# Moving a product with C from GpSimd to VectorE in a 16-layer Mamba kernel, with the five engines' lists reordered

## The reference, cut to what matters

```python
H, I, N, R, K, NL = 192, 384, 16, 48, 4, 16      # width, channels, states, dt rank, conv taps, layers
def selective_scan(u, dt, A, Bm, Cm, Dp):
    def step(h, inp):
        u_t, dt_t, B_t, C_t = inp
        dA = jnp.exp(dt_t[:, :, None] * A)
        h = dA * h + (dt_t * u_t)[:, :, None] * B_t[:, None, :]
        y = jnp.einsum('bin,bn->bi', h, C_t)
        return (h, y)
    ...
    return jnp.moveaxis(ys, 0, 1) + u * Dp
def mamba_layer(x, p):
    h = rmsnorm(x, nw)
    u, z = jnp.split(jnp.einsum('blh,ch->blc', h, in_w), 2, axis=-1)
    u = jax.nn.silu(causal_conv(u, cw, cb))
    proj = jnp.einsum('bli,ci->blc', u, xp_w)
    dt_r, Bm, Cm = (proj[..., :R], proj[..., R:R + N], proj[..., R + N:])
    dt = jax.nn.softplus(jnp.einsum('blr,ir->bli', dt_r, dtw) + dtb)
    y = selective_scan(u, dt, -jnp.exp(a_log), Bm, Cm, dp) * jax.nn.silu(z)
    return x + jnp.einsum('bli,hi->blh', y, ow)
```

## Time and profile before

| what | value |
|---|---|
| time, median of 3 runs | 14570.39 us (14560.91 to 14575.47) |
| the profiled execution's own time | 14539.11 us |
| its span | 14537.1 us |
| mean granted TensorE clock | 0.929 of full |
| stage of the layers | about 200 us to 13412 us of the span |
| VectorE, GpSimd, TensorE, ScalarE busy | 89%, 87%, 87%, 78% of the span |

### The profile page before, as it was taken

How to read it: one execution, slowest core, us unless ns; L and a number is a source line. 1 busy time by engine, 2 the same in 40 slices (tenths; PEclk the granted TensorE clock), 3 DMA queues, 4 the chain that set the end, 5 groups by cost and what they waited for, 6 DMA issues and landing times. The chain is left out here.

```text
span 14537.1 us, 203073 instructions
## 1 busy us (share of the span) xinstructions
PE 12640.6 (87%) x51466; PEld 6492.0 (45%) x51466; DVE 12997.2 (89%) x8757; ACT 11405.9 (78%) x21744; POOL 12668.3 (87%) x6352
## 2 busy tenths in 40 slices
PE   7888888888888888888888888888888888888989
PEld 4444444444444444444444444444444444444767
DVE  3999999999999999999999999999999999998633
ACT  4888888888888888888888888888888888888211
POOL 2999999999999999999999999999999999998033
PEclk8999999999999999999999999999999999999899
DMA  3555555555555555555555555555555555555022
GB/s 103 149 154 151 150 156 152 159 150 155 148 154 151 149 156 152 156 152 156 149 152 151 149 155 150 157 150 157 152 154 149 149 155 150 156 150 155 26 65 57
DMA packets 825576, 2086.15 MB, mean 144 GB/s; under 512 B 101243, under 2 KB 381308, under 8 KB 825336
## 3 DMA queue, kind: packets, MB, share of 16 engines
q1 hardware_dynamic: 693720, 1684.45, 34.2%
q0 software_dynamic: 130992, 399.73, 14.8%
q10 hardware_dynamic: 720, 0.55, 0.0%
HBM read 1414.20 MB, written 286.41 MB: 117 GB/s over the span
## 5 line engine op out<-in xcount | busy, mean ns | idle before, releaser
L911 POOL TENSOR_TENSOR dbu<-dtu_rep,b_rep 128x972 f32<-128x972 f32 x4096 | 9634.8, 2529 | 624.5 <-DVE h L846 617.7
L846 DVE TENSOR_TENSOR_SCAN h<-ps,dbu 128x972 f32<-128x972 f32 x4096 | 8769.2, 2169 | 442.9 <-ACT ps L646 417.3
L646 ACT ACTIVATE ps<-dt_rep,A_cur 128x323 f32<-128x323 f32 x12288 | 5864.2, 521 | 201.6 <-DVE h L846 156.5
L479 PE MATMUL ps<-h,fold 128*32 128x486 f32 x16400 | 3699.4, 632 | 2.1 <-DVE h L855 2.1
L855 DVE TENSOR_TENSOR h<-h,ps 128x972 f32<-128x972 f32 x3329 | 3681.1, 1149 | 0.3 <-DVE ps L1204 0.3
L557 PE MATMUL ps<-u_raw,w_cv 128*128 128x162 f32 (+7 forms) x8256 | 1827.5, 374 | 170.2 <-ACT u_raw L682 168.9
L919 POOL TENSOR_TENSOR h<-h,c_rep 128x972 f32<-128x972 f32 x769 | 1945.5, 2530 | 0.0
L557 PEld LDWEIGHTS ps<-u_raw,w_cv 128*128 128x128 f32 x8256 | 1337.6, 190 | 731.4 <-ACT u_raw L682 299.3
L466 PE MATMUL ps<-c_rows,sel_c 16*128 16x324 f32 x2048 | 989.4, 568 | 747.7 <-DVE h L855 747.7
L479 PEld LDWEIGHTS ps<-h,fold 128*32 128x32 f32 x16400 | 746.3, 115 | 1981.7 <-issue 1977.0
L508 PE MATMUL ps<-x_norm,w_z 96*128 96x324 f32 (+1 forms) x4112 | 1177.3, 435 | 1.4 <-ACT rstd L715 0.7
(11 more groups left out here) (186 smaller groups left out, 12683.8 us busy)
## 6 DMA issues: line engine op xcount, KB each, us to landing
dtu_rep<-dtu_rows SPq DMA_DIRECT2D x1028, 486.0 KB, 4.6
dt_rep<-dt_rows SPq DMA_DIRECT2D x1028, 486.0 KB, 5.2
b_rep<-b_rows SPq DMA_DIRECT2D x1028, 162.0 KB, 4.9
dt<-exp_x POOLq DMA_DIRECT2D x257, 486.0 KB, 5.3
dt<-dtu POOLq DMA_DIRECT2D x257, 486.0 KB, 4.4
dt<-u_pre POOLq DMA_DIRECT2D x257, 486.0 KB, 4.5
dt_rows<-dt SPq DMA_DIRECT2D x257, 486.0 KB, 2.7
dtu_rows<-dtu SPq DMA_DIRECT2D x257, 486.0 KB, 2.9
```

What stands on the lines that cost most here:

```text
L479: mm = pe.matmul(y_ps[32 * r:32 * r + 32, half, :], fold[:, :], src[:, half * YW:(half + 1) * YW], start=(m in (0, 1)), stop=(m < 0))
L646: ins = act.activation(decay[s % 2][:, it * L + 1:(it + 1) * L], dt_rep[:, s % NR, it, 1:L], ACT.Exp, scale=A_cur[:, it * N + s:it * N + s ...
L846: dve.tensor_tensor_scan(h[s % RING][:, :, :].rearrange("p i t -> p (i t)"), decay[s % 2], dbu[s % DRING][:, :, :].rearrange("p i t -> p ( ...
L911: pool.tensor_tensor(dbu[s % DRING][:, :, :], dtu_rep[:, r, :, :], b_rep[:, q, :].unsqueeze(1).broadcast_to([128, IT, L]), ALU.mult).then_ ...
```

## The change

`ON_POOL` goes from three states (3, 7, 12) to two (4, 12). All that depends on it follows: `c_rep` has two slots in place of three, and one C load fewer is issued per unit. The lists of all five engines are put in another order. The diff, with the parts that only close or open an `if` shortened:

```diff
-ON_POOL = (3, 7, 12)
+ON_POOL = (4, 12)
...
     p, k, j = u + 1, u + 2, u + 3
     te_ss(pe, j, b1)
+    te_sum(pe, u, -2)
     te_bcast(pe, u, par, 0)
-    te_sum(pe, u, -2)
     te_z(pe, p, 1 - par, 0)
...
     te_sum(pe, u, 1)
     te_u(pe, k, par, 1, scan, b1)
+    te_skip(pe, u, par, 0)
+    te_skip(pe, u, par, 1)
     te_conv(pe, k, 0)
     te_bcast(pe, u, par, 2)
     te_conv(pe, k, 1)
-    te_skip(pe, u, par, 0)
-    te_skip(pe, u, par, 1)
     te_sum(pe, u, 2)
+    te_sum(pe, u, 3)
     te_xp(pe, k, par)
-    te_sum(pe, u, 3)
+    te_sum(pe, u, 4)
     te_dt(pe, k, 0)
...
     te_dt(pe, k, 1)
-    te_sum(pe, u, 4)
     te_sum(pe, u, 5)
...
     other = 1 - par
     se_copy_A(act, u)
+    se_softplus(act, p, 0)
     se_decay(act, u, 0)
     se_decay(act, u, 1)
-    se_softplus(act, p, 0)
     act.preload_act_table_set(LOG_SET)
     se_log_ss(act, j)
...
     se_decay(act, u, 2)
-    se_c_rows(act, p, other)
     se_z(act, p, 0)
-    se_copy_nw(act, j)
     se_decay(act, u, 3)
     se_z(act, p, 1)
     se_decay(act, u, 4)
+    se_decay(act, u, 5)
+    se_out(act, u, 0)
     se_softplus(act, p, 2)
-    se_decay(act, u, 5)
-    se_out(act, u, 0)
+    se_softplus(act, p, 3)
+    se_sq(act, j + 1)
+    se_copy_nw(act, j)
     se_decay(act, u, 6)
     se_out(act, u, 1)
+    se_decay(act, u, 7)
+    se_weighted_x(act, j, other)
-    se_softplus(act, p, 3)
-    se_decay(act, u, 7)
-    se_rstd(act, j)
+    se_c_rows(act, p, other)
     se_ur(act, k, 0)
-    se_weighted_x(act, j, other)
     se_decay(act, u, 8)
+    se_decay(act, u, 9)
     se_ur(act, k, 1)
-    se_decay(act, u, 9)
+    se_copy_cb(act, k)
+    se_rstd(act, j)
     se_decay(act, u, 10)
-    se_copy_cb(act, k)
     se_conv(act, k, 0)
     se_decay(act, u, 11)
-    se_sq(act, j + 1)
     se_decay(act, u, 12)
     se_conv(act, k, 1)
...
     ve_product(dve, u, -1)
     ve_scan(dve, u, 0)
+    ve_product(dve, u, 0)
     ve_scan(dve, u, 1)
-    ve_product(dve, u, 0)
-    ve_product(dve, u, 1)
     ve_scan(dve, u, 2)
     ve_gate(dve, u, other)
     ve_scan(dve, u, 3)
+    ve_product(dve, u, 1)
     ve_scan(dve, u, 4)
+    ve_product(dve, u, 2)
+    ve_product(dve, u, 3)
     ve_scan(dve, u, 5)
-    ve_product(dve, u, 2)
     ve_scan(dve, u, 6)
-    ve_product(dve, u, 4)
+    ve_scan(dve, u, 7)
     ve_product(dve, u, 5)
-    ve_scan(dve, u, 7)
+    ve_product(dve, u, 6)
     ve_scan(dve, u, 8)
-    ve_product(dve, u, 6)
+    ve_product(dve, u, 7)
     ve_scan(dve, u, 9)
     ve_scan(dve, u, 10)
+    ve_product(dve, u, 8)
     ve_scan(dve, u, 11)
-    ve_product(dve, u, 8)
     ve_product(dve, u, 9)
+    ve_scan(dve, u, 12)
     ve_product(dve, u, 10)
     ve_product(dve, u, 11)
-    ve_scan(dve, u, 12)
     ve_scan(dve, u, 13)
     ve_scan(dve, u, 14)
+    ve_product(dve, u, 13)
     ve_scan(dve, u, 15)
-    ve_product(dve, u, 13)
     ve_product(dve, u, 14)
...
     ge_dbu(pool, u, 0)
     ge_dbu(pool, u, 1)
     ge_dbu(pool, u, 2)
-    ge_dbu(pool, u, 3)
     ge_dt(pool, p, 1 - par, 0)
+    ge_dbu(pool, u, 3)
     ge_dbu(pool, u, 4)
     ge_dbu(pool, u, 5)
     ge_dbu(pool, u, 6)
-    ge_dbu(pool, u, 7)
     ge_dt(pool, p, 1 - par, 2)
-    ge_product(pool, u, 3)
+    ge_dbu(pool, u, 7)
     ge_dbu(pool, u, 8)
     ge_dt(pool, p, 1 - par, 1)
     ge_dbu(pool, u, 9)
     ge_dbu(pool, u, 10)
-    ge_x_norm(pool, u + 3, 1 - par)
+    ge_product(pool, u, 4)
+    ge_dbu(pool, u, 11)
     ge_dt(pool, p, 1 - par, 3)
-    ge_dbu(pool, u, 11)
     ge_dbu(pool, u, 12)
     ge_dbu(pool, u, 13)
-    ge_product(pool, u, 7)
     ge_dbu(pool, u, 14)
     ge_dbu(pool, u, 15)
+    ge_x_norm(pool, u + 3, 1 - par)
     def sp_store_b(sp, k, par):
...
     def sync_step(sp, u, par, scan=True, a1=True, b1=True, reload=None):
     p = u + 1
-    sp_load_c(sp, u, par, 2)
     sp_load_b(sp, u, par, 0)
     sp_store_dt(sp, p, 0)
...
     reload(1)
     sp_load_b(sp, u, par, 1)
+    sp_load_c(sp, u, par, 1)
+    sp_load_dt(sp, u, 0)
+    sp_load_c(sp, p, 1 - par, 0)
     sp_load_dtu(sp, u, 0)
     sp_load_dtu(sp, u, 1)
-    sp_load_dt(sp, u, 0)
+    sp_store_b(sp, u + 2, par)
     sp_load_dt(sp, u, 1)
+    sp_load_dt(sp, u, 2)
     sp_load_dtu(sp, u, 2)
     sp_load_dtu(sp, u, 3)
     reload(2)
-    sp_load_dt(sp, u, 2)
     sp_load_dt(sp, u, 3)
     sp_load_b(sp, u, par, 2)
-    sp_store_b(sp, u + 2, par)
     sp_load_b(sp, u, par, 3)
-    sp_load_c(sp, p, 1 - par, 0)
-    sp_load_c(sp, p, 1 - par, 1)
     reload(3)
...
```

More of the change, by code:

```diff
@@ L614, in tensor_step @@
                 te_u(pe, k, par, 1, scan, b1)
+            if scan:
+                te_skip(pe, u, par, 0)
+                te_skip(pe, u, par, 1)
+            if a1:
                 te_conv(pe, k, 0)
@@ L772, in scalar_step @@
                 se_copy_A(act, u)
+            if b1:
+                se_softplus(act, p, 0)
+            if scan:
                 se_decay(act, u, 0)
                 se_decay(act, u, 1)
-            if b1:
-                se_softplus(act, p, 0)
             act.preload_act_table_set(LOG_SET)
@@ L793, in scalar_step @@
                 se_decay(act, u, 4)
+                se_decay(act, u, 5)
+                se_out(act, u, 0)
             if b1:
                 se_softplus(act, p, 2)
+                se_softplus(act, p, 3)
+            se_sq(act, j + 1)
+            se_copy_nw(act, j)
             if scan:
-                se_decay(act, u, 5)
-                se_out(act, u, 0)
                 se_decay(act, u, 6)
                 se_out(act, u, 1)
+                se_decay(act, u, 7)
+            se_weighted_x(act, j, other)
             if b1:
-                se_softplus(act, p, 3)
-            if scan:
-                se_decay(act, u, 7)
-            se_rstd(act, j)
+                se_c_rows(act, p, other)
             if a1:
                 se_ur(act, k, 0)
-            se_weighted_x(act, j, other)
             if scan:
                 se_decay(act, u, 8)
+                se_decay(act, u, 9)
             if a1:
                 se_ur(act, k, 1)
+                se_copy_cb(act, k)
+            se_rstd(act, j)
             if scan:
-                se_decay(act, u, 9)
                 se_decay(act, u, 10)
             if a1:
-                se_copy_cb(act, k)
                 se_conv(act, k, 0)
@@ L1056, in sync_step @@
             if b1:
-                sp_load_dt(sp, u, 2)
                 sp_load_dt(sp, u, 3)
                 sp_load_b(sp, u, par, 2)
-            if a1:
-                sp_store_b(sp, u + 2, par)
-            if b1:
                 sp_load_b(sp, u, par, 3)
-                sp_load_c(sp, p, 1 - par, 0)
-                sp_load_c(sp, p, 1 - par, 1)
             if reload:
```

## The result

| | kernel before | changed kernel |
|---|---|---|
| median | 14571.80 us (4 runs) | 14458.42 us (4 runs, 14427.27 to 14463.64) |
| ratio | | 0.9915, 95% interval 0.9903 to 0.9928 |
| profiled execution, its span | 14539.11, 14537.1 us | 14463.64, 14461.6 us |

The changed kernel is faster by 0.85%, 113 us. The forecast was 408 us, and 14162 with a range that ended at 14300. The measured time lies outside it.

What follows compares the result with a forecast made beforehand. Bound: VectorE's list plus handoff stalls, 51.2 us a unit. Floor 49.35 plus 0.25 stall gives 49.6; 1.6 saved times 255 units is 408 us, so 14570 becomes 14162, range 14085 to 14300.

Steps and rivals of the forecast that it cites:

- The floor: VectorE's list of 16 scans, 14 products and a gate without any stall: 49.35 us a unit.
- the handoffs: VectorE's waits for other engines: stalls at the gate and scan 4 go, 0.25 us stays at scan 13.
- The walk: Stepping through the engines' new lists over one unit, at full clock, to find remaining stalls; gave 49.6 us a unit.
- The stall before the gate: VectorE's wait for TensorE's sum of states 14 and 15, 1.08 us a unit; was to go with 2 us to spare.
- The 0.25 us above the floor: Stall before scan 13, as ScalarE's chain of copy, SiLU and table loads makes decay 13 late; range 0 to 0.6.
- GpSimd has slack: GpSimd's list fills 45 to 46 us of a unit, leaving 3.5 us; nothing of VectorE waits for it, cost 0.
- D: Rival, slower: SyncE's dt_rep 1 load behind the store makes decay 1 and scan 2 late; 14750 us, chance 0.04.
- So I take full clock: TensorE before the broadcast: idle stretch cut from 2.62 to about 1.2 us, so granted clock stays 1.00 in the layers.
- Rival B: Clock still falls at the first broadcast; gate 0.5 us later, unit 50.1 us, time 14290; chance 0.12.
- the constant offset: 31 us by which the shown median of the kernel before exceeds its profiled execution, added to 14131 to give 14162.
- C: Rival: handoffs make decays 2, 7 and 13 each 0.3 us late; unit 50.3 to 50.6, about 14380; chance 0.10.
- E: Rival, no gain: stalls of 1.6 to 1.9 us reappear where the walk doesn't see; 14570, chance 0.02.

Runs made afterwards that it cites:

- run 8: Changed kernel plus four idle matmuls (fillers) a unit on TensorE: two before the x projection, one before each half of the dt projection; 14209.65 us.
- run 5: Changed kernel with SyncE's list of the kernel before, the store of B and C rows behind the dt_rep and dtu_rep loads; 14446.39 us.
- Run 1: Changed kernel plus two idle matmuls (fillers) on TensorE before the x projection; 14267.34 us, ratio 0.9788.
- Runs 1, 7 and 8: Changed kernel with two, three and four fillers; the middle one adds to Run 1 a filler before dt half 1: 14222.73 us.
- run 10: Control: changed kernel plus one idle matmul before the second half of the u projection; 14471.37 us, ratio 0.9922.
- run 3: Kernel before, with its old split and lists, plus three idle matmuls before its first broadcast; 14285.13 us, ratio 0.9805.
- run 4: Kernel before with the split alone: one product a unit moved from GpSimd to VectorE, other lists as before; 14590.89 and 14592.12 us.

## Why the prediction was wrong, point by point

**The floor: right; the handoffs: mostly.** The walk gave 49.6; the shortest units take 49.63, and in run 8 nearly every unit takes 49.74. The stall before the gate went. The 0.25 us above the floor lies elsewhere than the walk had it: no idle time before scan 13 passes 0.15 us in any unit. In the unit from 1425.70, scan 13 starts 0.1 us late, and product 0 starts 2.28 us after scan 0 (1467.80 to 1470.08) where 2.09 is usual. That the two come to nearly the 0.25 of the forecast is luck. GpSimd has slack, as said: it waits 746 us for `dtu_rep` 2, which the forecast called 2 us late and absorbed, and run 5 shows that it costs nothing. D and its price did not occur.

**The step that failed: "So I take full clock".** The forecast had the granted clock at 1.00 throughout the layers; it was 0.94, against 0.93 before. The step rested on a bound of 1.37 us for an idle piece that leaves the clock alone, and on TensorE's longest idle piece being under 1.5 us. Both were wrong.

- The idle piece before the x projection is 1.85 to 2.18 us in the layers. The prediction has no figure for it in the new list, only the 1.37 of the kernel before. It lacked that the sums of states 4, 5 and 6, 7 side by side take as long as one: 1.85 us for 16 matmuls in the rows above. The kernel before shows it too (sums 4 and 5, its eight-matmul rows being 1.83):

```profile
6024.47 1.85 PE L479 MATMUL ps<-h,fold 128*32 128x486 f32 x16
```

  A sum writes two of four groups of 32 output rows, and the next one the other two. The Trainium skill (TensorEngine Tiling (Array Packing), Tiling Modes) lists 128x32 as four independent tiles; the trace agrees, with 1.85 against 1.83 us. The new list also takes the skip products (1.81 us together) out of this place.
- The length of one idle piece doesn't decide. Run 1 shows a fall behind 0.26 and 0.61 us, and in the changed kernel the clock stayed up behind 2.14 us in the unit from 1425.70. Rival B had the clock fall behind short pieces, but placed it at the first broadcast and priced it at 0.5 us of every unit. It came mostly at the x and dt projections, in four units of five, at 1.0 or 2.4 us.

In terms of the sum: from first gate to last the layers were to gain 408 us and gained 135 (13099.7 - 12964.4), which is 273 less. Runs 1, 7 and 8, which change nothing but the fillers, gave 234 of that back: the last gate went from 13270.3 to 13036.2 us. The one filler of run 10, put where no low stretch follows, gave nothing. That low stretches over the x and dt projections are what lengthens the units is shown so; why the clock falls in one unit and not in the next, behind the same idle piece, is open.

**Why it was faster at all.** The forecast had the gain come from stalls that the new lists remove. But in run 3 the old lists lose the stalls at the gate and before scan 4 when the clock is up, and then take 49.31 a unit, 0.32 less than the new ones at their best. What the change gained is that its low stretches cost less: 50.67 - 49.63 = 1.04 us a unit in the mean, against 51.20 - 49.31 = 1.89. These are units of different runs, so this is worked out and not tried by itself. By it, the right sign was in part luck.

**A second term, that was not in the forecast: what follows the layers.** Span less start of the last gate is 14461.6 - 13270.3 = 1191.3 us, and 14537.1 - 13404.9 = 1132.2 in the kernel before, though no instruction of that part was changed. TensorE's clock over it:

```profile
13405.00:14537.00 1132.00, 1015.35 (x5086) 0.91 0.22 51
```
```profile
13270.00:14462.00 1192.00, 1058.02 (x5088) 0.88 0.21 49
```

In the other profiled runs this part took 1162 to 1195 us, never 1132. So the profiled execution of the kernel before was a lucky one there, and the 31 us between it and the median need not be the constant offset that was carried over. 273 + 59 make the 332 us between 14131 and 14463.6. The length of this part goes with its clock: 0.91 over 1132 us, 0.90 in the four profiles of 1162 to 1168 us, 0.88 in the four of 1191 to 1195. What decides that clock in an execution was not tried.

**The rivals.** C named stalls at decays 2, 7 and 13 and a unit of 50.3 to 50.6. Scan 2 is late in 141 units and scan 15 in 148, decays 7 and 13 in none; the waits for decays (65 us in all) follow the clock, since they vanish in run 8. E, stalls in places that the walk doesn't see, had a chance of 0.02; such stalls came, before product 0 and scan 15, and with those before scan 2 they took most of the gain, though not all.

## What to carry to other kernels

Where TensorE is 87% busy but made of short products with waits between them, work out a changed order at both clock levels, and take the trace of before as evidence for the clock only where the order stays the same. In such a kernel a filler in a wait off the critical path can be worth more than a search over lists: here 249 us against 113 from the whole change. It must be placed by the map of those low stretches that cost time, checked again after each addition, and kept off the queue of the product that is needed next.

## What was not expected of the hardware

- The clock goes low with little idle time: behind idle pieces of 0.26 and 0.61 us in run 1, and 0.9 us after the end of an idle piece of 2.15 us in the changed kernel. It can also stay up behind 2.14 us.
- The units of one program can alternate: 50.38 us without a low stretch and 52.02 with two, in run 4.
- A low stretch may cost nothing: all 50 short units of the changed kernel have one.
- More work made the program faster: run 8 has 4 fillers a unit, 0.74 us each, 3 us of added TensorE work, and takes 249 us less than the changed kernel (362 us less than the kernel before: 14571.80 and 14209.65).
